# RWKV and gated experts on one core: reciprocal roots of the end on GpSimd, end reordered

## The reference, cut to what matters

```python
def attn(hidden):                      # hidden: (8, 512, 512), fp32
    shifted = pad(hidden, one step)[:, :-1]
    key, value, rec = (hidden * m + shifted * (1 - m) for m in mixes)
    k, v, r = key @ Wk, value @ Wv, sigmoid(rec @ Wr)
    return r * wkv(time_decay, time_first, k, v) @ Wo     # a scan over time
def ffn(x):                            # E = 8 experts of width I = 16, top 2
    gate = softmax(x @ router_w.T) masked to its top 2
    h = silu(einsum('bth,eih->beti', x, down_w))
    return einsum of h with up_w, weighted by gate
x = layernorm(x + attn(x))             # layernorm: (x - mean) / sqrt(var + 1e-5)
x = layernorm(x + ffn(x))
```

## Time and profile before

| | us |
|---|---|
| median of 3 runs | 455.28 (455.16 to 455.67) |
| profiled execution, whole | 455.12 |
| its span, first to last instruction | 453.3 |
| TensorE busy | 442.3 |
| VectorE busy | 404.6 |
| ScalarE busy | 363.7 |
| GpSimd busy | 313.0 |

### The profile page before, as it was taken

One profiled execution on the slowest core, in us unless ns is written; L12 is line 12 of the kernel. 1 busy time (PEld: TensorE's weight loads), 2 busy tenths in 40 slices (PEclk: granted clock), 3 DMA queues, 4 the chain that ended last, 5 costly groups with the idle time before them and its releaser, 6 DMA issues. The chain is left out here.

```text
span 453.3 us, 6683 instructions
## 1 busy us (share of the span) xinstructions
PE 442.3 (98%) x1984; PEld 340.7 (75%) x1984; DVE 404.6 (89%) x614; ACT 363.7 (80%) x810; POOL 313.0 (69%) x298
## 2 busy tenths in 40 slices
PE   8999999999999999999999999999999999999993
PEld 3444667778888888888888888888888888878771
DVE  6999999898888989999899989999899996875985
ACT  7877668877888779888788789888789887668695
POOL 0455786688657997579867898579966794753335
PEclk9999999999999999999999999999999999999998
DMA  8603320042000042003320042100520023400016
GB/s 250 217 1 119 116 69 1 1 140 72 0 1 0 25 163 88 6 0 99 113 71 0 1 158 78 45 0 25 163 94 0 4 68 94 140 1 0 1 48 231
DMA packets 20244, 30.64 MB, mean 68 GB/s; under 512 B 2032, under 2 KB 7152, under 8 KB 20208
## 3 DMA queue, kind: packets, MB, share of 16 engines
q1 hardware_dynamic: 20064, 29.95, 20.5%
q10 hardware_dynamic: 144, 0.26, 0.2%
HBM read 21.82 MB, written 8.39 MB: 67 GB/s over the span
## 5 line engine op out<-in xcount | busy, mean ns | idle before, releaser
L604 ACT ACTIVATE PR<-PR 128x512 f32<-128x512 f32 x128 | 74.5, 582 | 29.0 <-DVE PR L948 9.6
L1255 POOL TENSOR_TENSOR DQ<-DEN,EX 128x512 f32<-128x512 f32 x32 | 41.9, 1310 | 23.6 <-DVE DEN L919 23.6
L1261 POOL TENSOR_SCALAR NM<-SUM,RS 128x1 f32<-128x1 f32 x30 | 7.9, 264 | 59.8 <-ACT RS L604 59.8
L342 PE MATMUL PK<-KH,WKH 128*128 128x512 f32 x112 | 46.5, 415 | 0.4 <-DVE NUM L936 0.4
L970 DVE SCALAR_TENSOR_TENSOR KT<-D,VEC,XT 128x512 f32<-128x512 f32 x56 | 46.3, 874 | 0.0
L342 PE MATMUL PV<-VH,WVH 128*128 128x512 f32 x112 | 45.4, 406 | 0.0
L342 PE MATMUL PR<-RH,WRH 128*128 128x512 f32 x112 | 44.3, 395 | 0.2 <-DVE RW L960 0.2
L348 PE MATMUL PK<-KL,WKH 128*128 128x512 f32 x112 | 44.1, 394 | 0.0
L348 PE MATMUL PV<-VL,WVH 128*128 128x512 f32 x112 | 44.1, 394 | 0.0
L348 PE MATMUL PR<-RL,WRH 128*128 128x512 f32 x112 | 44.0, 393 | 0.0
L343 PE MATMUL PK<-KH,WKL 128*128 128x512 f32 x112 | 43.8, 391 | 0.0
(11 more groups left out here) (289 smaller groups left out, 1276.0 us busy)
## 6 DMA issues: line engine op xcount, KB each, us to landing
XT<-in_xt SPq DMA_DIRECT2D x32, 256.0 KB, 3.7
XN<-in_x SPq DMA_DIRECT2D x28, 256.0 KB, 2.7
out<-XN SPq DMA_DIRECT2D x28, 256.0 KB, 2.0
X1T<-in_wo SPq DMA_DIRECT2D x1, 1024.0 KB, 5.5
XT<-in_x SPq DMA_DIRECT2D x4, 256.0 KB, 3.6
out<-XT SPq DMA_DIRECT2D x3, 256.0 KB, 2.3
X1T<-in_wk SPq DMA_DIRECT2D x2, 256.0 KB, 5.0
XN<-in_wv SPq DMA_DIRECT2D x2, 256.0 KB, 5.5
```

The source lines that it names most:

```text
L342: eng.matmul(dst[:, :], wh[:, c, o], high[:, c, :], start=(c == 0), stop=False)
L604: eng.activation(*a, **k).then_inc(q[s], 1)
L1255: eng.tensor_tensor(DQ[:, :], DEN[:, 0:T], EX[:, 1, :], ALU.add).then_inc(q["e"], 1)
L1261: eng.tensor_scalar(NM1[:, col(t)], total, RS1[:, col(t)], scale, ALU.mult, ALU.mult)\
```

## The change

1. **Roots on GpSimd.** A tile POWER of two columns holds -0.5. For the tiles of `MEASURED1`, `normalise` now makes the reciprocal root itself: a `tensor_scalar` add of eps, then a `tensor_tensor` with the operation pow. For the whole end of the second layernorm GpSimd has a `root2` of the same two instructions; ScalarE keeps only the squares (`square2`), whose scale now includes 1/H. Twelve tiles of the end get their second root so, in eight `root2` calls.
2. **End reordered.** On TensorE `ffn_up(t5)` stands behind the projection of t7 + 3, and the `turn` and `hidden` of the last tiles stand ahead of `ffn_turn(LAST - 1)` and of the ups. On ScalarE and VectorE copies and gates follow the same order; VectorE's `silu` is cut in two. Banks and waits are changed to fit.
3. **Start.** All four key mixes of batch 1 are made in slot 0, and WKL is made by GpSimd in slot 0, in four instructions, once those mixes are done.

The diff, cut to its core:

```diff
-        sb("GAP0", [128, 48])
+        POWER = sb("POWER", [128, 48])[:, 0:2]
...
-            return tail_bank(t, PU, PT, PK[0], PU) if t // NT == LAST - 2 else PU[:, :]
+            return tail_bank(t, PU, PH, PK[0], PU) if t // NT == LAST - 2 else PU[:, :]
...
@@ ffn_up (TensorE)
-                if b == LAST and n == 0:
-                    eng.wait_ge(q["res2"], NT * (LAST - 2) + 2)
-                elif b == LAST and n == NT - 1:
+                if b == LAST and n == NT - 1:
...
                 elif b == LAST - 2 and 0 < n < NT - 1:
-                    eng.wait_ge(q["res"], NT * LAST + 1 + n)
+                    eng.wait_ge(q["res"], NT * LAST + 5 - n)
...
@@ end of TensorE's block
-            ffn_up(t5)
             project_high(t7 + 3)
             project_low(t7 + 3)
             project_rest(t7 + 3)
+            ffn_up(t5)
             turn(t7)
-            ffn_turn(LAST - 1)
+            ffn_up(t5 + 1)
             turn(t7 + 1)
             hidden(t7)
-            ffn_up(t5 + 1)
             turn(t7 + 2)
+            ffn_turn(LAST - 1)
             hidden(t7 + 1)
-            ffn_up(t5 + 2)
             turn(t7 + 3)
             hidden(t7 + 2)
+            ffn_up(t5 + 2)
+            hidden(t7 + 3)
             ffn_up(t5 + 3)
-            hidden(t7 + 3)
...
@@ end of ScalarE's block
             spread(t7)
-            spread(t7 + 1)
+            spread(t7 + 2)
             turned(t7)
-            spread(t7 + 2)
-            ffn_out(LAST - 1)
-            spread2(t5)
             turned(t7 + 1)
             hidden_copy(t7)
-            spread(t7 + 3)
             turned(t7 + 2)
+            ffn_out(LAST - 1)
             hidden_copy(t7 + 1)
             ffn_in(LAST)
             turned(t7 + 3)
             hidden_copy(t7 + 2)
-            spread2(t5 + 1)
-            square2(t5 + 2, JUNK[:, :])
+            square2(t5)
             hidden_copy(t7 + 3)
             ffn_in(LAST + 1)
+            square2(t5 + 2)
             ffn_out(LAST)
-            square2(t5 + 3, KT[:, 0, :])
-            root2(t5 + 2, 2)
+            square2(t5 + 3)
             ffn_out(LAST + 1)
-            spread2(t6, 2)
-            spread2(t6 + 2, 2)
-            spread2(t7, 2)
-            spread2(t7 + 2)
-            spread2(t7 + 3)
+            for t in range(t6, t7 + 2):
+                square2(t)
...
@@ VectorE's block
-                if s < 2:
-                    mixes(1, 0, 2 * s, 2 * s + 1)
+                if s == 0:
+                    mixes(1, 0, 0, 1, 2, 3)
...
-                if s < 2:
-                    low_weights(2 * s)
...
             residual(t7)
-            silu(LAST - 1)
             residual(t7 + 1)
             moments(t7 + 1)
             residual(t7 + 2)
-            residual2(t5)
+            silu_of(LAST - 1)
             residual(t7 + 3)
             moments(t7 + 3)
+            silu_gated(LAST - 1)
+            residual2(t5)
             residual2(t5 + 1)
             moments2(t5 + 1)
             gate_scores(LAST)
+            gate_top(LAST)
+            silu_of(LAST)
+            silu_gated(LAST)
             residual2(t5 + 2)
-            gate_top(LAST)
-            silu(LAST)
             residual2(t5 + 3)
             gate_scores(LAST + 1)
...
@@ GpSimd's block
+            def root2(t, n):
+                cols = slice(col(t).start, col(t).start + n)
...
+                eng.tensor_scalar(LV2[:, cols], spread, EPS, None, ALU.add).then_inc(q["lv2"], n)
+                eng.wait_ge(q["lv2"], t + n)
+                eng.tensor_tensor(RS2[:, cols], LV2[:, cols], POWER[:, 0:n], ALU.pow).then_inc(q["rs2"], n)
...
+                if s == 0:
+                    eng.wait_ge(q["kt"], 3 * C + C)
+                    low_weights(0, *range(C))
...
-            for n in range(NT - 1):
+            for n in range(NT):
                 normalise(t7 + n)
+            root2(t5, 1)
             normalise2(t5)
-            normalise(t7 + 3)
-            for t in range(t5 + 1, NT * NB):
-                if t not in FINISHED:
-                    normalise2(t)
+            root2(t5 + 1, 1)
+            normalise2(t5 + 1)
+            for t in (t5 + 2, t6, t6 + 2, t7):
+                root2(t, 2)
+                normalise2(t)
+                normalise2(t + 1)
+            root2(t7 + 2, 1)
+            root2(t7 + 3, 1)
```

More of the change, by code:

```diff
@@ L337, in split @@
                     eng.wait_ge(q["hw"], which + 1)
-                    eng.wait_ge(q[("lwk", "lwv", "lwr")[which]], j + 1 if which else 2)
+                    eng.wait_ge(q[("lwk", "lwv", "lwr")[which]], j + 1)
                 for c in range(C):
@@ L651, in spread @@
             def spread(t):
[L652 to L662, removed]
+                eng.wait_ge(q["res"], t + 1)
+                act("sq1", JUNK[:, :], xn_at(t), ACT.Square, bias=SUM1[:, col(t)], scale=-float(H),
+                    accum_out=SQ1[:, col(t)])
+                eng.wait_ge(q["sq1"], squared(t, MEASURED1))
+                act("lv1", LV1[:, col(t)], SQ1[:, col(t)], ACT.Ln, bias=EPS, scale=float(H) ** -3)
+                eng.wait_ge(q["lv1"], squared(t, MEASURED1))
                 act("rs1", RS1[:, col(t)], LV1[:, col(t)], ACT.Exp, scale=-0.5)
@@ L678, in spread2, with square2 @@
                 eng.activation(RS2[:, cols], LV2[:, cols], ACT.Exp, scale=-0.5).then_inc(q["rs2"], n)
-            def square2(t, junk):
+            def square2(t):
+                i = squared(t, MEASURED)
+                eng.wait_ge(q["sq2"], i - 2)
                 eng.wait_ge(q["res2"], t + 1)
[L682 to L689, removed]
+                act("sq2", (JUNK[:, :], KT[:, 0, :])[i % 2], xn_at(t), ACT.Square, scale=float(H) ** -0.5, accum_out=SQ2[:, col(t)])
             def turned(t):
@@ L1071, in silu, with silu_gated @@
                 eng.tensor_tensor(p.tiled(p.s1), p.tiled(p.s1), p.hs[:, :, 0:EI], ALU.mult).then_inc(q["sh"], 1)
+            def silu_gated(k):
+                p = PARTS[k]
                 eng.wait_ge(q["sh"], k + 1)
@@ L1193, in _ @@
             gate_top(LAST + 1)
-            silu(LAST + 1)
+            silu_of(LAST + 1)
+            silu_gated(LAST + 1)
             for n in range(NT):
@@ L1259, in normalise @@
                 total, scale = (SUM1[:, col(t)], -1.0 / H) if i is None else (MV[:, 5 + i, 0:1], -1.0)
-                eng.wait_ge(q["rs1"], t + 1)
+                if i is not None:
+                    eng.wait_ge(q["mv1"], i + 1)
+                    eng.tensor_scalar(LV1[:, col(t)], MV[:, 5 + i, 1:2], EPS, None, ALU.add).then_inc(q["lvp"], 1)
+                    eng.wait_ge(q["lvp"], i + 1)
+                    eng.tensor_tensor(RS1[:, col(t)], LV1[:, col(t)], POWER[:, 0:1], ALU.pow).then_inc(q["rsp"], 1)
+                    eng.wait_ge(q["rsp"], i + 1)
+                else:
+                    eng.wait_ge(q["rs1"], squared(t, MEASURED1))
                 eng.tensor_scalar(NM1[:, col(t)], total, RS1[:, col(t)], scale, ALU.mult, ALU.mult)\
@@ L1265, in normalise @@
                    .then_inc(q["nrp"], 1)
+            def root2(t, n):
+                cols = slice(col(t).start, col(t).start + n)
+                if t in MEASURED:
+                    i = MEASURED.index(t)
+                    eng.wait_ge(q["mv2"], i + n)
+                    spread = MV[:, i:i + n, 1]
+                else:
+                    eng.wait_ge(q["sq2"], squared(t + n - 1, MEASURED))
+                    spread = SQ2[:, cols]
+                eng.tensor_scalar(LV2[:, cols], spread, EPS, None, ALU.add).then_inc(q["lv2"], n)
+                eng.wait_ge(q["lv2"], t + n)
+                eng.tensor_tensor(RS2[:, cols], LV2[:, cols], POWER[:, 0:n], ALU.pow).then_inc(q["rs2"], n)
             def normalise2(t):
@@ L1278, in low_weights @@
             def low_weights(i, *blocks):
-                stage, high, low, done = ((XN[0], WVH, WVL, "lwv"), (XN[1], WRH, WRL, "lwr"))[i - 1]
+                stage, high, low, done = ((X1T, WKH, WKL, "lwk"), (XN[0], WVH, WVL, "lwv"), (XN[1], WRH, WRL, "lwr"))[i]
                 eng.wait_ge(q["hw"], i + 1)
```

21 lines of the change are left out of this document (9 added, 12 removed).

## The result

The changed kernel takes 461.48 us (median of 4 runs, 461.26 to 461.61); the kernel before, timed beside it, 455.33 us (4 runs, 455.16 to 455.67). The ratio is 1.0132, with a 95% interval of 1.0118 to 1.0146: 1.3% slower. The forecast was 459.3 us, with a range of 457.6 to 463.0. So the direction and the range held, but the loss is 6.15 us where 4.0 was worked out. The profiled execution took 461.26 us, with a span of 459.5; before it was 455.12 and 453.3.

What follows compares the result with a forecast made beforehand. TensorE's pace was taken to bound the kernel until the end, where a chain to the last store sets the time. 455.12 + 0.18 (start) + 3.84 (GpSimd's root queue) = 459.14, median 459.3 us; range 457.6 to 463.0.

Steps and rivals of the forecast that it cites:

- line of pairs begins: End, GpSimd: its queue of paired normalisations with roots was to begin at 442.56 us, where it began at 442.15.
- four pairs with roots: End, GpSimd: each pair with an add and a power takes 2.26 us, four take 9.04, ending at 451.60.
- two last roots: End, GpSimd: roots of t7 + 2 and t7 + 3 behind the pairs, 0.63 us each, ending at 452.86.
- The rival of a dear power: GpSimd's power takes 0.9 us or more, giving 463.1 up to 465.5 us; chance 0.13.
- the second hidden product: End, TensorE: without waiting for ScalarE it starts at about 432.7 us instead of 433.25, 0.58 earlier.
- the last gate block: End, VectorE: starts at 439.14 us instead of 438.75, 0.39 later, behind the sum of t5 + 3.
- the transpose at 430.56 stays, within 0.1: End, TensorE, tile t7 + 1: GpSimd's own root, two steps of 0.37 us, fills the former 0.89 us idle time.
- the place of the ups: End, TensorE: ups of t5 + 3 move behind the last hidden product, done at 438.51 us instead of 437.23.
- the start's term: Slot 0, VectorE: 0.18 us more work is handed on to TensorE's wait for NUM; +0.18, between 0 and +0.5.
- A pause at the power's first use: Rival at the root of t7 + 1, about 428.8 us: 0.9 us pause gives 460.2, several us 462 or more; chance 0.03.
- GpSimd keeps up: Rival in the end: a root costs GpSimd 0.07 us or less, time down to 454.9 us; chance 0.05.
- roots overlap: Rival in the end: small steps partly overlap; at half price 457.1 us, nearly all hidden 455.7; chance 0.09.

Runs made afterwards that it cites:

- the start alone: Kernel before with only the start's edits (all four key mixes in slot 0, WKL by GpSimd): 454.94 us, ratio 0.9993.

## Why the prediction was right, and where its size was off

**The mechanism held.** The last scaling waits for GpSimd's root and not for the variance; the line has no gap; ScalarE is idle for 8.64 us, more than the 6 named. Where the scaling was forecast at 452.96, it starts at 456.01. The 3.05 us between come apart so:

| step of the sum | worked out | trace of after | difference |
|---|---|---|---|
| line of pairs begins | 442.56 | 443.41 | +0.85 |
| four pairs with roots | 9.04 | 10.73 (443.41 to 454.14) | +1.69 |
| two last roots | 1.26 | 1.83 (454.14 to 455.97) | +0.57 |
| from the last root to the scaling | 0.10 | 0.04 | -0.06 |

**The price of the power was mis-sized.** It was taken as 0.26 us, the price of a small step of the same width. It is 0.71 for two columns and 0.57 for one. Its bounds, 0.10 and 1.30, held it. The exchange for a multiplication shows that the operation itself is dear: without it the line ended at 452.80, and the forecast had 452.86 (a coincidence: there a later beginning, 443.11 against 442.56, and cheaper roots cancel). The choice of "the step of the same width in the trace" took no account of the operation. The rival of a dear power began at 0.9 us; the measured price lies between the forecast's and that.

**Some luck in the number.** The upper end of the forecast itself, 461.5, was worked out with a power of 0.6 (which by the sum gives 461.3) and with the gate block in time. The power of two columns is above 0.6 and the gate block was late, and 461.48 still lies inside, because 0.87 us went the other way (the sum below). One of the prediction's own signs of being wrong, "power rows of well over 0.3 us", came true. Of its signs of being right, three failed: the second hidden product is later and not earlier, the last gate block is not at 439.1, and TensorE's wait for NUM did not grow (below).

**The gate block was 0.80 later than worked out.** The step that failed is "the transpose at 430.56 stays, within 0.1". It moved to 431.10. The two small steps were priced at 0.37 us from start to start; the add took 0.61 to the next row (428.54 to 429.15) and the power 0.67 (to 429.82), 0.54 more together. The power's 0.30 of this is the same mistake as above. The add's 0.24 is another one: its row is 0.53 long beside VectorE's product of 427.96, where the add of t7 + 3 (432.57) takes 0.22. A second collision had no term either: VectorE's product of 430.45 stretched `NM` of t7 + 2 to 0.69, and the transposes behind it came 0.23 later than TensorE could have made them. A further 0.14 is a slip in the sum, which starts from 430.42, the end of GpSimd's row, and not from TensorE's own 430.56. These are 0.91 together, and the steps behind give 0.11 back. From the second hidden product on the steps hold: 3.91 us to the last hidden product (3.98 worked out), 0.92 to the ups (0.91), 3.47 from the gate block to the line (3.42). The runs put the first roots, to which the sum gave no cost, at 0.90 us, and the place of the ups, for which it had 0.97 (from 0.58 early to 0.39 late), at 1.03.

**The start.** Most of its steps held, and its sign did not. WKL's lows ran from 25.92 for 4.97 us, the denominator behind them from 30.84 for 1.27, and the reader stands at 32.83: hidden, as said. Most of the 0.18 us is there as well: from the gate product of slot 0 to the scan behind it the kernel before takes 3.70 us (22.15 to 25.85), the start alone 3.85 (22.12 to 25.97), and these 0.15 are handed on through 27 slots, to the scans at 384.08 and 384.19. The way into TensorE was another: its wait for NUM stayed at 0.43 instead of growing to 0.6, and a new wait of 0.22 appeared ahead of it, in all kernels with the new start:

```profile
56.77 3.67 PE L391 MATMUL PP<-X1T,RW 128*128 128x512 f32 x8 [0.22 <-DVE RW L960]
```

What the sum left out is the instruction behind the scan at 384.19: there the shorter list of VectorE saves a wait of 0.46 us, and the chain comes out 0.2 us ahead. Measured over runs, the term is between -0.7 and +0.1 us, not +0.18.

**The sum closed.** From the forecast for the profiled execution, 459.14, to the measured 461.26 it is 2.12 us: 3.05 for the scaling, less 0.18, since the start's term had been added to the scaling's time while the measured time holds its effect already, less 0.69 for the end behind the scaling (kept at 4.2, now 3.5), less 0.06 outside the span. That stretch goes with the queue: it is 3.4 to 3.8 us in the five kernels with the second roots on GpSimd and 4.2 to 4.7 in the nine others. That fewer transfers are still under way then would explain it; this is argued, not shown.

**The other rivals.** A pause at the power's first use is not seen: the first at 429.15 takes 0.57 us and the second, at 432.87, 0.56; the rule of the Trainium skill (GPSIMD Engine Reference, Instruction dispatch) on freshly loaded kernels does not show for the power here. That GpSimd keeps up, or that roots overlap, is refuted by rows without a gap.

**What stays open.** Why a place in VectorE's list costs half a microsecond: the runs show that it goes by the place, not what happens there. And in the profiled executions slot 0 begins up to 0.5 us earlier or later, before any edit acts (22.12 to 22.61 for the same product); sizes below that are read from stretches within one trace.

## What to carry to other kernels

An engine's idle time is no proof that it can take a step: look at where in its queue the step would stand, and who waits for what is behind. Here a root cost ScalarE two steps of 0.2 us between its squares, while on GpSimd the last tile's root stood behind eight normalisations that its scaling did not need. And an operation that no row shows is priced by its kind before its width: a power is not an add, and where six of them stand on the path, the value belongs between the bounds and not at the cheapest neighbour.

## What the runs showed of the hardware

- A `pow` of GpSimd takes 0.56 to 0.58 us for one column of 128 partitions and 0.71 for two, so 0.14 more for the second column; a multiplication takes 0.19 for either. (The last one of the list takes longer in both kernels, 0.65 and 0.30.)
- VectorE's product of two SBUF tiles and GpSimd's work hinder each other. In the kernel after, GpSimd's normalisations start 0.28 and 0.26 us ahead of VectorE's products (427.68 and 427.96, 430.19 and 430.45) and keep their 0.77 or 0.76, while the products take 1.02 and 1.03 instead of 0.69; GpSimd's small steps behind take 0.53 and 0.69 instead of 0.22 and 0.27. With the residual moved, GpSimd's row starts only 0.11 us ahead (428.75 and 428.86); there the product takes 0.69 and the normalisation 1.28. The Trainium skill (SBUF — State Buffer, Who interferes with whom) says that an instruction of VectorE with two SBUF inputs contends with a GpSimd instruction that reads SBUF, and that the order of issue decides who blocks. These rows agree that they contend and that one of them goes on undisturbed; the order of their starts alone does not tell which, since GpSimd's row is the earlier one in all three pairs. Moving such a product in the order gained nothing, since the cost went to the other engine.
- VectorE has a wait that belongs to a place in its list of instructions and not to the work there: 0.46 us at one product of slot 27 (0.27 at the scan ahead of it when two tiny instructions were added before), at the 832nd instruction each time. Removing two instructions 360 us earlier took it away. In the traces this moves the end by 0.2 us, which is 0.05% and less than the runs here can tell.
